# Three edits around the second attention layer: a subtraction on another engine, a second bank, function tables loaded ahead

## The reference, cut to what matters

```python
k = jnp.einsum('ihd,bpd->biph', W_K, x)
q = jnp.einsum('ihd,bpd->biph', W_Q, x)
v = jnp.einsum('ihd,bpd->biph', W_V, x)
scores = jnp.einsum('biph,biqh->biqp', k, q)
masked = scores * mask - 1e10 * (1.0 - mask)
attn = jax.nn.softmax(masked / jnp.sqrt(d_head), axis=-1)
z = jnp.einsum('biqp,biph->biqh', attn, v)
z_flat = jnp.transpose(z, (0, 2, 1, 3)).reshape(b, pos, -1)
out = jnp.einsum('df,bqf->bqd', W_O, z_flat)
```

## Time and profile before

| | us |
|---|---|
| median of 3 runs | 690.08 |
| lowest, highest run | 689.97, 695.9 |
| the profiled execution's own time | 690.88 |
| its span in the trace | 689.0 |

### The profile page before, as it was taken

One profiled execution on the slowest core, in us unless ns is written; L12 is line 12 of the kernel. 1 busy time (PEld: TensorE's weight loads), 2 busy tenths in 40 slices (PEclk: granted clock), 3 DMA queues, 4 the chain that ended last, 5 costly groups with the idle time before them and its releaser, 6 DMA issues.

```text
span 689.0 us, 16437 instructions
## 1 busy us (share of the span) xinstructions
PE 673.7 (98%) x4363; PEld 606.2 (88%) x4363; DVE 575.8 (84%) x1757; ACT 439.9 (64%) x1738; POOL 361.1 (52%) x555
## 2 busy tenths in 40 slices
PE   8999999999999998999998999999999999999998
PEld 4789999999999997888886999999999999878887
DVE  6879999999899999878964898989898998796433
ACT  4888888888788886431436766666666666654222
POOL 5998888898889863201047953415142324027000
PEclk9999999999999999999999999999999999999999
DMA  7010210101020010100024657565656556300000
GB/s 244 2 48 8 102 48 2 47 0 46 1 107 31 31 50 29 47 0 1 16 91 102 138 118 168 107 147 121 141 117 147 128 126 141 70 1 1 1 30 32
DMA packets 131117, 48.02 MB, mean 70 GB/s; under 512 B 96752, under 2 KB 126064, under 8 KB 130928
## 3 DMA queue, kind: packets, MB, share of 16 engines
q1 hardware_dynamic: 107024, 34.89, 21.0%
q10 hardware_dynamic: 24032, 12.46, 6.1%
HBM read 34.67 MB, written 12.65 MB: 69 GB/s over the span
## 4 chain that ended last, share of the span: by engine, by line
PE 87%; DVE 6%; issue 2%; ACT 2%; DMA 1%; SPq 0%; POOL 0%; ACTq 0%; DVEq 0%; POOLq 0%
PE bank L513 12%; PE bank L521 12%; PE bank L951 12%; PE bank L410 11%; PE bank L540 6%; PE bank L378 5%; PE bank L442 5%; PE bank L448 4%; PE bank L371 4%; PE bank L1025 3%; PE bank L463 3%; PE bank L424 3%; PE bank L1029 3%; PE bank L1045 1%; DVE x L706 1%
## 5 line engine op out<-in xcount | busy, mean ns | idle before, releaser
L706 DVE SCALAR_TENSOR_TENSOR x<-bank,rinv,x 128x256 f32<-128x256 f32 x256 | 121.2, 473 | 2.3
L684 ACT ACTIVATE probs<-scores,negmax 128x128 f32<-128x128 f32 (+1 forms) x256 | 117.7, 473 | 5.4 <-DVE negmax L753 4.4
L593 ACT CAST enc_hi<-bank 128x256 fp32r<-128x256 f32 x128 | 47.8, 373 | 81.8 <-PE bank L448 79.5
L836 POOL TENSOR_TENSOR a_hi<-raw_a,zero 128x384 fp32r<-128x384 f32 (+1 forms) x60 | 43.6, 727 | 73.9 <-PE bank L540 73.9
L314 POOL TENSOR_TENSOR ln_r<-ln_ve,neg_half 128x1 f32<-128x1 f32 x26 | 17.0, 654 | 118.5 <-DVE ln_ve L288 118.5
L717 DVE TENSOR_TENSOR enc_lo<-bank,enc_hi 128x256 fp32r<-128x256 f32 x128 | 54.0, 422 | 28.3 <-PE bank L378 17.1
L410 PE MATMUL bank<-b_hi,enc_hi 128*128 128x256 f32 x256 | 73.4, 287 | 0.5 <-DVE x L706 0.5
L410 PE MATMUL bank<-b_lo,enc_hi 128*128 128x256 f32 x256 | 72.4, 283 | 0.0
L410 PE MATMUL bank<-b_hi,enc_lo 128*128 128x256 f32 x256 | 72.3, 283 | 0.0
L854 POOL TENSOR_TENSOR rot_a<-rot_a,rot_b 128x384 f32<-128x384 f32 x64 | 64.8, 1012 | 8.3 <-DVE rot_b L824 6.8
L852 POOL TENSOR_TENSOR rms_r<-meansq,neg_half 128x3 f32<-128x3 f32 x64 | 54.8, 856 | 7.4 <-DVE negmax L753 2.2
(11 more groups left out here) (185 smaller groups left out, 2372.1 us busy)
## 6 DMA issues: line engine op xcount, KB each, us to landing
shuffle<-blocks ACTq DMA_DIRECT2D x59, 192.0 KB, 2.5
arrived<-shuffle SPq DMA_DIRECT2D x236, 48.0 KB, 2.2
raw_a<-in_wa SPq DMA_DIRECT2D x40, 192.0 KB, 3.1
raw_a<-in_wa SPq DMA_DIRECT2D x9, 512.0 KB, 4.3
raw_b<-in_wb SPq DMA_DIRECT2D x16, 256.0 KB, 2.7
hid_last<-in_wax SPq DMA_DIRECT2D x2, 512.0 KB, 4.9
w_a<-in_w2t SPq DMA_DIRECT2D x1, 1024.0 KB, 4.7
raw_b<-in_wdown SPq DMA_DIRECT2D x2, 512.0 KB, 3.2
```

The costliest lines, as they stand in the source:

```text
L593: nc.scalar.copy(enc[0][:, hh, b * D:(b + 1) * D], bank[O_BANK][:, 0:D]).then_inc(s["ehi"], 1)
L684: nc.scalar.activation(probs[:, c % 4, c0:c1], scores[:, c % 2, c0:c1], ACT.Exp, bias=negmax[:, c % 2, r:r + 1], scale=-1.0, accum_out=row ...
L706: nc.vector.scalar_tensor_tensor(out=x[:, m % 8, :], in0=output_bank(m)[:, hh * D:(hh + 1) * D], scalar=rinv[:, u, r:r + 1], in1=x[:, m % ...
```

## The change

Three parts.

1. The low part of layer 1's turned probabilities is subtracted on GpSimd (`pool_turned_lo`), as the first thing of its slot, no more on VectorE. Both operands lie in SBUF.
2. Layer 1's value projection alternates between banks 4 and 5 (`v_bank`); PE's waits ahead of it are for the eviction of the tile before the last. The first probabilities that PE turns into bank 5 wait for all evictions (unit 59). Layer-norm tile 6 moves from bank 5 to bank 4, with waits for the evictions of value tile 2.
3. ScalarE runs a one-column activation whose result nobody reads at three places, so that its table is loaded there: Silu in `act_drain0` (t = 2, layer 0's drain), Exp in layer 1's head behind slot -1, Silu behind layer 1's last slot (t = 7). At the kernel's start ScalarE waits for `zero`, which these read.

```diff
+        def v_bank(m):
+            return bank[(TQ_BANK, PT_BANK)[m % 2]]
@@ pe_turn_probs
+                if L == 1 and m == MOVED:
+                    pe.wait_ge(s["vev"], UNITS)
@@ pe_slot, value projection of tile m = c + 5
-                    need(pe, s["vev"], it, m)
-                    need_pairs(pe, s["vlo"], it, (m + 1) // 2, 4)
+                    need(pe, s["vev"], it, m - 1)
+                    need_pairs(pe, s["vlo"], it, m // 2, 4)
-                        mm = pe.matmul(bank[TQ_BANK][:, 0:D], xT[l][:, g, t * P:(t + 1) * P],
+                        mm = pe.matmul(v_bank(m)[:, 0:D], xT[l][:, g, t * P:(t + 1) * P],
@@ act_slot (and the same in dve_slot's low part)
-                    src = bank[TQ_BANK][:, 0:D]
+                    src = v_bank(m)[:, 0:D]
@@
+        def pool_turned_lo(pool, it, m):
+            s = at[1]
+            if live(it, m) and in_parts(1, it, m):
+                need(pool, s["ptev"], it, m + 1)
+                nc.gpsimd.tensor_tensor(turned[1][:, 1, m % 2, :], arrived[:, m % 4, 0:256], turned[1][:, 0, m % 2, :].bitcast(F32),
+                                        ALU.subtract).then_inc(s["ptlo"], 1)
@@ dve_slot
-                dve_turned_lo(dve, L, it, c - 3)
+                if L == 0:
+                    dve_turned_lo(dve, it, c - 3)
@@ pool_slot
             s = at[L]
+            if L == 1:
+                pool_turned_lo(pool, it, c - 3)
             if L == 0:
@@
-        LN2_BANK = (2, 3, 4, 5, 6, 7, 5, 6)
+        LN2_BANK = (2, 3, 4, 5, 6, 7, 4, 6)
@@
+        def act_function_ahead(act, function):
+            nc.scalar.activation(unused[:, :], zero[:, :], function)
@@ act_drain0, behind slot UNITS + t
+                elif t == 2:
+                    act_function_ahead(act, ACT.Silu)
@@ ScalarE's start
+            act.wait_ge(s_zero, 1)
             act.wait_ge(raw_as[0][0], 16)
@@ ScalarE's head
+                    elif L == 1 and c == -1:
+                        act_function_ahead(act, ACT.Exp)
@@ ScalarE's tail
+                    if L == 1 and t == 7:
+                        act_function_ahead(act, ACT.Silu)
@@ PE's head
                     elif L == 1 and c == -2:
-                        pe.wait_ge(ln["lo"], 20)
+                        pe.wait_ge(at[1]["vev"], 3)
+                        pe.wait_ge(at[1]["vlo"], 2)
                         ln_pe(pe, 2, 6, LN2_BANK[6])
```

More of the change, by code:

```diff
@@ L177, in build @@
         zero = sb("zero", [P, 1])
+        unused = sb("unused", [P, 1])
         neg_half = sb("neg_half", [P, TILES])
@@ L718, in dve_enc_lo, with dve_turned_lo @@
                                         ALU.subtract).then_inc(s["elo"], 1)
-        def dve_turned_lo(dve, L, it, m):
-            s = at[L]
-            if live(it, m) and in_parts(L, it, m):
+        def dve_turned_lo(dve, it, m):
+            s = at[0]
+            if live(it, m) and in_parts(0, it, m):
                 need(dve, s["ptev"], it, m + 1)
-                src = arrived[:, m % 4, 0:256] if L == 1 else bank[PT_BANK][:, 0:256]
-                nc.vector.tensor_tensor(turned[L][:, 1, m % 2, :], src, turned[L][:, 0, m % 2, :].bitcast(F32),
+                nc.vector.tensor_tensor(turned[0][:, 1, m % 2, :], bank[PT_BANK][:, 0:256], turned[0][:, 0, m % 2, :].bitcast(F32),
+                                        ALU.subtract).then_inc(s["ptlo"], 1)
[4 more added lines that the diff above has]
+                nc.gpsimd.tensor_tensor(turned[1][:, 1, m % 2, :], arrived[:, m % 4, 0:256], turned[1][:, 0, m % 2, :].bitcast(F32),
                                         ALU.subtract).then_inc(s["ptlo"], 1)
@@ L810, in dve_slot @@
                     need(dve, s["vev"], it, m + 1)
-                    nc.vector.tensor_tensor(v_part(1, 1, m // 8 % 2, t // 2), bank[TQ_BANK][:, 0:D],
+                    nc.vector.tensor_tensor(v_part(1, 1, m // 8 % 2, t // 2), v_bank(m)[:, 0:D],
                                             v_part(1, 0, m // 8 % 2, t // 2).bitcast(F32), ALU.subtract).then_inc(s["vlo"], 1)
```

## The result

| | us |
|---|---|
| before, median of 20 runs | 691.26 |
| after, median of 20 runs (lowest, highest) | 695.53 (694.74, 698.57) |
| after / before | 1.0045, 95% interval 1.0031 to 1.006 |
| after, the profiled execution's own time, its span | 695.38, 693.6 |

The change costs 4.3 us between the medians and 4.5 us between the profiled executions. The prediction had 3.6. Its 693.7 us for the median stood on the 690.08 of three runs; over 20 runs the kernel before has 691.26, so 1.2 of the 1.8 us by which 693.7 was too low are the base.

What follows compares the result with a forecast made beforehand. PE was taken to bound the kernel, without slack in layer 1's loop. GpSimd's queue at +3.9 us, less 0.3 for shorter butterfly steps, gave +3.6: 693.7 us for the median, range 687.0 to 696.4.

Steps and rivals of the forecast that it cites:

- What bounds it: Layer 1's loop: PE has no idle time, so only making it wait or taking its work moves the end.
- Part 3: Subtraction moved to GpSimd: its full queue in slots 5 to 10 delays unit 8's value product by 3.9 us.
- The term that I had chosen at 0.3: Slots 5 to 10: butterfly steps shorten without VectorE's subtraction beside them; 0.3 us off, at most 0.8.
- X: Start of GpSimd's full run ahead of the loop, at the subtraction of unit 2, forecast at 375.45 us.
- The start: Kernel start: ScalarE's new wait on `s_zero` stands ahead of a copy already waiting for its weights; cost 0.
- Part 2: Two-bank value projection: 3.41 us of gaps in slots 1 to 4 vanish; unit 2's value product about 3.7 us earlier.
- Part 1: Function tables loaded ahead: Exp load hidden before slot 0, ScalarE gains 1.30 us; both Silu loads gain 0.
- T in the loop hidden: Loop: GpSimd's subtraction of 0.73 us fits the 4.5 us available, so PE does not wait for it.
- rival D: Loop: subtraction late behind weight splits, 0.5 us each for 5 pairs, 696.2 us; chance 0.04.
- B: Each subtraction costs 1.04 us on GpSimd: +6.1 us, 696.2 us; chance 0.12.
- C: Layer 1's head: the Exp table isn't loaded ahead, 695.0 us; chance 0.08.
- Rival A: Head: GpSimd's queue doesn't hold PE, value products stay 3.6 us early, 686.5 us; chance 0.13.

Runs made afterwards that it cites:

- e5: The kernel before with one added line, ScalarE's wait for `zero` ahead of its first copy; 692.24 us, ratio 1.0.
- e1: The changed kernel with ScalarE's wait for `zero` moved behind its first copy; 694.93 us, ratio 1.0037.
- e9: The kernel before with only the one-column Exp ahead, its wait for `zero` behind the first copy; 689.74 us, ratio 0.9972.
- e7: e1 with the subtraction on VectorE ahead of the loop and on GpSimd in the loop; 688.01 us, ratio 0.9921.
- e2: e1 with the subtraction back on VectorE throughout; 689.43 us, ratio 0.9952.
- e6: e1 with GpSimd's six butterfly steps moved from slots 5 to 10 to behind slots 59 to 64; 688.54 us, ratio 0.9952.
- e8: e6 with the butterfly steps two each behind slots 59 to 61; 687.47 us, ratio 0.9917.
- e4: The kernel before with only the value projection in two banks, with the layer-norm tile's bank; 688.62 us, ratio 0.9946.
- e3: The kernel before with only the subtraction moved to GpSimd; 697.17 us, ratio 1.0071.
- e11: e7 with the butterfly steps where e8 has them, behind slots 59 to 61; 687.06 us, ratio 0.9925.
- e10: e2 with the butterfly steps where e8 has them, behind slots 59 to 61; 689.57 us, ratio 0.9957.

## Why the prediction was right, and where it was not

- **What bounds it: right.** PE ran without idle time from 411 to 588, and V(8)'s delay, 4.44 us, is the whole difference to the end (4.52).
- **Part 3, the queue of GpSimd in slots 5 to 10: right in mechanism, its size too high by 1.1 us.** From T(2)'s start to T(8)'s end I had 28.35 + 7 x 0.73 - 0.3 = 33.2 us; it took 32.02. The term that I had chosen at 0.3 between 0 and 0.8 should have stood at its upper end: the steps took 2.40 us (2.36 to 2.41) instead of 2.52, 6 x 0.12 = 0.7 us, once VectorE's T was gone. T itself stands 0.70 us apart from what follows it, not 0.73: another 0.2. The last 0.4 are in the two 512-wide pieces, which also got shorter (2.53 and 2.59 us each in before, 2.34 and 2.36 in after), and which the prediction carried over as they were. In time the jam cost 409.31 - 1.46 - 404.87 = 3.0 us, not 3.6 (T(2) came 0.1 us later than X plus the late start, PE starts 0.24 us behind T(8), and the 405.04 that I had counted from is 0.17 behind V(8)'s first matmul).
- **The start: wrong.** "ScalarE's new wait on `s_zero` ... stands ahead of a copy that waits for its weights' transfer anyway: 0." The copy does wait, but the table load that the copy needs does not, as long as nothing stands ahead of it; I left out an instruction that the program's text doesn't show and the trace does. It cost 1.46 us at V(8) (e5), and at the entry 1.4 (e5 against before) to 1.8 us (after against e1).
- So the sum of 3.6 comes near by two misses that partly cancel: 3.0 for the jam and 1.5 for the start make the 4.4 measured at V(8). That it is off by no more than 0.8 is luck in part.
- **PE's lower clock behind its gaps: not in the prediction.** It was free in after. In e1 it took 0.6 us of the 1.4 by which T(8) came earlier (V(8) at 408.5 instead of 407.9). That e1's V(8) in the chain, 408.63, meets the predicted 408.64 is chance, not the sum.
- **Part 2, V(2) 3.7 us earlier: right.** It started at 378.18 against 380.60 in the rows of PE, with 1.46 us of the late start in it: 3.9. Its ground was incomplete: 1.27 of the 3.41 us of gaps go with the table load alone as well (e9), so Parts 1 and 2 both claim them.
- **Part 1, Exp ahead: right.** Hidden, 0.42 us to spare in after, gain for ScalarE 1.4 us (the first Exp starts at 362.05 against 362.00, with 1.46 us of the late start in it); the one-column activation took 0.20 us where I allowed 0.40. The two Silu loads gained nothing, as said: after is 1.46 us late ahead of the first feed-forward and 1.46 behind it, 4.52 where the second's matmuls start and 4.6 at the end of the span.
- **T in the loop hidden: right.** No PE gap at line 449 there (e7 and e2 alike), so rival D is out; T at 0.72 to 0.75 us ahead of the loop rules B out; the load at 359.15 rules C out. Rival A, that GpSimd's queue doesn't hold PE, is what e6 and e8 make true by moving the queue, and its 3.6 us are what they show: V(8) at 401.4 to 401.6.
- **Signs foretold:** idle in slots 8, 10 and 11 of about 1, 3.6 and 2.6 us; found 0.58, 3.10 and 0.68 (and 0.50 in slot 6). The last is small since PE came late to it, at the lower clock.

What stays open: why executions of one kernel differ by up to 8 us. In before the mean granted clock of an execution goes from 0.993 to 1.0 and the spans from 695.7 down to 687.9, but not in step (one with 1.0 has a span of 692.4); of e4, 10 of 11 executions have 1.0 and lie within 686.2 and 687.2. That the one-bank gaps make PE's clock fall in some executions of before, and that part of e4's gain is this, fits (e3's profiled execution has the lower clock behind that gap, before's has not) and was not shown. That a gap is followed by the lower clock was seen in after, e1 and e3, not in e7, and not varied by itself.

## What to carry to other kernels

Before work goes to an engine that is half idle, read that engine's queue in the stretch where the result is first wanted: a share of 52% held a run of 28 us without a gap, and a step of 0.7 us put at the head of each slot inherited all of it. Then either leave the work where it was in the stretch that is full (e7), or move the filler work out of that stretch (e6, e8); here both cured the loss. The move itself brought nothing from V(8) on but in one case, beside the late butterfly (e11 against e10). And a wait is placed not only ahead of the instruction that it is for but ahead of everything the compiler puts in front of that instruction, a table load among it.

## What the runs showed of the hardware

- T, a VectorE instruction with two SBUF operands, ends 0.3 us behind a long GpSimd instruction that it starts beside: it took 2.28 us beside a butterfly step of 2.37 (e7), 2.48 beside the first of two in a row (e10), 1.68 in e4, 0.42 alone. `xn`, a `TENSOR_SCALAR` with one wide SBUF operand, took 1.67 instead of 0.41 (e6) and ended 0.16 us behind the step. The Trainium skill ("SBUF — State Buffer", SBUF: two separate sides) says that the pair of ports which the two engines share is locked for a whole instruction and that the other engine blocks until then; the trace agrees.
- GpSimd's own loss from it is small: 2.52 us a step in before, 2.40 with T gone from VectorE.
- PE's granted clock was at the lower level behind gaps of 3.10, 2.96 and 2.20 us (0.50 in after, 0.64 over 8 us in e1, 0.57 over 4 us in e3); behind a gap of 1.91 us in slot 4 of e3 it was 0.55 to 0.60 over 376 to 380. Behind the same gap of before, 1.79 us, and behind one of 2.11 us in e7 it stayed at 1.00 in the profiled executions, so the length of the last gap alone does not decide it.
- A table load inside the kernel took 1.28 us and, in e9, no more than 0.02 us of idle time on ScalarE ahead of it and behind it.
